# Where the column sums of an arccos attention are taken: ScalarE's accumulator or VectorE

## What is computed

```
cos = jnp.einsum('bhsd,bhtd->bhst', q, k)
g_dist = jnp.arccos(jnp.clip(cos, -1.0 + EPS, 1.0 - EPS)) * SPHERE_RADIUS
attn_score = (1.0 + g_dist / BANDWIDTH ** 0.5) ** (-D_INTRINSIC - ALPHA)
n_r = jnp.sum(attn_score, axis=-1)
n_c = jnp.sum(attn_score, axis=-2)
k_tilde = (n_r ** (-A))[..., :, None] * attn_score * (n_c ** (-A))[..., None, :]
probs = k_tilde / jnp.maximum(jnp.sum(k_tilde, axis=-1, keepdims=True), 1e-12)
out = jnp.einsum('bhst,bhtd->bhsd', probs, v)
```

## Time and profile before

| | us |
|---|---|
| median of 3 runs (5336.09 to 5336.95) | 5336.46 |
| the profiled execution | 5337.28 |
| its span in the trace | 5335.6 |
| ScalarE busy | 4923.4 (92%) |
| VectorE busy | 3274.6 (61%) |
| TensorE matmul busy | 3097.5 (58%) |
| GpSimd busy | 1808.4 (34%) |

### The profile page before, as it was taken

One profiled execution on the slowest core, in us unless ns is written; L12 is line 12 of the kernel. 1 busy time (PEld: TensorE's weight loads), 2 busy tenths in 40 slices (PEclk: granted clock), 3 DMA queues, 4 the chain that ended last, 5 costly groups with the idle time before them and its releaser, 6 DMA issues. The chain is left out here.

```text
span 5335.6 us, 38170 instructions
## 1 busy us (share of the span) xinstructions
PE 3097.5 (58%) x10678; PEld 796.3 (15%) x10678; DVE 3274.6 (61%) x3861; ACT 4923.4 (92%) x2159; POOL 1808.4 (34%) x545
## 2 busy tenths in 40 slices
PE   7635565554444555444546657565655656565699
PEld 4200010000000000000001102111111111111244
DVE  7735665556545565545657676666767576666466
ACT  5799999999999999999989999999999999999521
POOL 0224433444334443334424443344333443334000
PEclk9866655667866656667566857686777668576799
DMA  2100000000000000000000101010010101010200
GB/s 87 63 8 14 18 14 14 14 18 18 14 18 16 12 10 10 6 6 10 12 29 24 36 10 52 2 51 10 30 32 24 36 10 51 7 47 2 82 28 16
DMA packets 71843, 128.14 MB, mean 24 GB/s; under 512 B 9654, under 2 KB 46937, under 8 KB 71706
## 3 DMA queue, kind: packets, MB, share of 16 engines
q1 hardware_dynamic: 70554, 122.50, 7.3%
q0 software_dynamic: 1152, 4.19, 0.3%
HBM read 96.77 MB, written 29.88 MB: 24 GB/s over the span
## 5 line engine op out<-in xcount | busy, mean ns | idle before, releaser
L1114 POOL TENSOR_TENSOR X<-X 128x2048 f32<-128x2048 f32 x504 | 1799.9, 3608 | 3001.3 <-DVE X L928 3001.3
L799 PE MATMUL psum<-stacks 128*128 128x512 bf16 x4096 | 1749.5, 524 | 1397.4 <-DVE X L942 1021.4
L942 DVE TENSOR_TENSOR X<-psum,X 128x1024 f32<-128x1024 f32 x1024 | 1194.3, 1218 | 1057.8 <-ACT X L1146 1046.5
L928 DVE TENSOR_SCALAR X<-psum 128x1024 f32<-128x1024 f32 x1024 | 1186.0, 1215 | 16.6 <-PE psum L799 13.9
L1168 ACT ACTIVATE X<-X 128x2048 f32<-128x2048 f32 x512 | 969.9, 1895 | 6.9
L1146 ACT ACTIVATE X<-X 128x4096 f32<-128x4096 f32 x256 | 904.8, 3604 | 0.7
L1138 ACT ACTIVATE X<-X,consts 128x8192 f32<-128x8192 f32 x128 | 903.7, 7107 | 0.0
L1154 ACT ACTIVATE X<-X 128x4096 f32<-128x4096 f32 (+1 forms) x192 | 897.8, 4739 | 2.7 <-DVE X L942 2.7
L1162 ACT ACTIVATE X<-X,consts 128x16384 f32<-128x16384 f32 x64 | 892.8, 13951 | 0.8
L824 PE MATMUL psum<-X,vp 128*32 128x512 f32 x4096 | 569.2, 715 | 474.1 <-DVE vp L953 473.8
L799 PEld LDWEIGHTS psum<-stacks 128*128 128x128 bf16 x4096 | 260.0, 105 | 2885.0 <-DVE X L942 1847.7
(11 more groups left out here) (165 smaller groups left out, 1347.4 us busy)
## 6 DMA issues: line engine op xcount, KB each, us to landing
V<-expert_w SPq DMA_DIRECT2D x64, 512.0 KB, 3.6
stacks<-qk_parts SPq DMA_DIRECT2D x256, 64.0 KB
qk_parts<-X SPq DMA_DIRECT2D x96, 128.0 KB, 1.9
stacks<-qk_parts SPq DMA_DIRECT2D x64, 192.0 KB
head_out<-evac SPq DMA_DIRECT2D x32, 256.0 KB, 2.1
expert_w<-u_t SPq DMA_DIRECT2D x17, 256.0 KB, 2.6
X<-in_L_attn_x_dram POOLq DMA_DIRECT2D x8, 512.0 KB, 4.3
stacks<-qk_parts SPq DMA_DIRECT2D x32, 128.0 KB
```

What stands on the lines that cost most here:

```text
L799: return nc.tensor.matmul(dst, stacks[:, 1, buf, keys:keys + P], stacks[:, 0, buf, q0:q0 + n], start=True, stop=True)
L928: nc.vector.tensor_scalar(X[:, m % 2, i, j * CW:(j + 1) * CW], ps_cos[j % 2], -CLIP, CLIP, ALU.max, ALU.min).then_inc(cos_ok, 1)
L942: nc.vector.tensor_tensor(part, ps_cos[j % 2], part, ALU.mult).then_inc(cos_ok, 1)
L1114: nc.gpsimd.tensor_tensor(own, own, own, ALU.mult).then_inc(square_ok, 1)
```

## The change

The Exp of the half-heads before the tail (`beside != "tail"`, k = 0 to 7) becomes one instruction for each half of the tiles, 128x8192, without an accumulator. For these half-heads VectorE takes the column sums itself: `values` gets a `reduce_sum` of 4 tiles of 2048 into 4 columns of `ncol`, with a semaphore `sums_ok` behind it for which the reciprocal waits. In the tail the Exp stays as it was; there VectorE raises `sums_ok` by itself, so that the count holds. ScalarE's wait on `vp_ok` stays only in the tail.

```
+        sums_ok = sem("sums_ok")
...
-                def values(k, m, piece):
+                def values(k, m, piece, own):
...
                     dve.wait_ge(score_ok, n * len(EXP_PIECES) + piece + 1)
+                    if own:
+                        nc.vector.reduce_sum(ncol[:, a:b], X[:, m % 2, a:b, :], AX.X).then_inc(sums_ok, 1)
+                    else:
+                        dve.sem_inc(sums_ok, 1)
+                    dve.wait_ge(sums_ok, n * len(EXP_PIECES) + piece + 1)
...
-                        values(k, m, piece)
+                        values(k, m, piece, beside != "tail")
...
-                def scores(k, m):
+                def scores(k, m, beside):
...
                     for piece, (a, b) in enumerate(EXP_PIECES):
-                        wait(act, vp_ok, n * len(EXP_PIECES))
+                        if beside != "tail":
+                            own = tiles(m, a, b)
+                            nc.scalar.activation(own, own, ACT.Exp, scale=POWER).then_inc(score_ok, 1)
+                            continue
+
+                        act.wait_ge(vp_ok, n * len(EXP_PIECES))
                         for i in range(a, b):
...
-                    scores(k, m)
+                    scores(k, m, beside)
```

## The result

The changed kernel takes **5293.62 us** (median of 4 runs, 5292.84 to 5294.67) against 5336.27 for the kernel before (4 runs): a ratio of 0.9919, 95% interval 0.9907 to 0.9932. The forecast was 5295, the range 5289 to 5310. The profiled execution took 5294.67 us, its span 5293.0.

A forecast was written before the change was run, and what follows sets the result against it. ScalarE was taken to bound the kernel before the tail. Saving 1.30 us on each of 32 half-heads, 41.6 us, from 5337.28 gave 5295.7 on the profiled execution, 0.8 above the median, so 5295 us; range 5289 to 5310.

The forecast's parts named there:

- ScalarE bounds the stretch before the tail: Half-heads before the tail: ScalarE busy 2289.69 of 2295.13 us, so a microsecond off its list is one off the time.
- The removed work is 15.15 us a half-head, the added 13.85: ScalarE's Exp before the tail: short Exp and reads occupy 15.15 us, two long Exp 13.85; saving 1.30 us per half-head.
- The third rival: ScalarE's Exp: the accumulator was worth its busy time, 2.62 us saved per half-head, 84 in all, 5253 us; chance 0.02.
- The fourth: Rival on ScalarE's long Exp: a cost stays for each row of 2048, saving 23 us, giving 5313 us; chance 0.02.
- The wait on vp_ok is worth nothing: ScalarE before the tail: no longer waiting on vp_ok gains nothing; all idle time ahead of 512 Exp is 6.9 us.
- A sum takes 8.7 us: VectorE before the tail: each of 64 sums of 8192 elements takes 8.7 us, at 1.04 ns an element.
- the bounds: Limits on one VectorE sum: 8.7 us from the slope between rows, at most 11.0 us if all 0.685 us were per element.
- The sums are hidden, with 3.3 us to spare: VectorE through TensorE to ScalarE's Arctan: products ready for it at E + 40.0 us, its own start at E + 43.3.
- No wait for GpSimd: VectorE's sums beside GpSimd's squares: one-operand sums do not wait; a wait would be 3.5 us, eating 6 us in all.
- The tail stays as it was: Tail: only a semaphore step by VectorE is added; ScalarE's waits there, 17.7 + 6.1 + 2.7 us, stay.
- The rule against tensor_reduce: VectorE's sums: the skill advises against tensor_reduce on a hot path; the prediction held this path is not hot before the tail.

## Why the prediction was right

- **ScalarE bounds the stretch before the tail.** Right: it has 2.8 us of idle time in 2252 there, and a turn lost what ScalarE's list lost.
- **The removed work is 15.15 us a half-head, the added 13.85.** Right to 0.01 us: 13.85 in the timeline. The third rival, which took busy times (2.62 us a half-head), would have given 5253. The fourth, a cost for each row of 2048 in the pattern, falls too: a long Exp takes 7.02 us, like the Arctan of the earlier trace rows.
- **The wait on vp_ok is worth nothing.** Wrong in size. A turn lost 74.04 - 72.66 = 1.38 us, not 1.30, and the 0.08 is the gap between Ln and Exp: 13.98 us now in every turn before the tail, 14.08 in the kernel before in the 28 half-heads inside the loops (13.98 in the four written out). There:

```profile
1527.77 13.95 ACT L1162 ACTIVATE X<-X,consts 128x16384 f32<-128x16384 f32 x1
```

  with the first Exp at 1541.85. The idle time ahead of Exp had stood in the view, 6.9 us for the whole span; I read it as nothing, and some 2.6 us of it went. So the 31 turns lost 2295.13 - 2252.32 = 42.8 us instead of 31 x 1.30 = 40.3. That the whole time fell by 42.7 us, only 1 more than the 41.6 forecast, is in part luck: the rest of the program gave back about 1.5 us, which was not followed up.
- **A sum takes 8.7 us.** Right: 8.678 to 8.687 for all 64. Between the bounds the slope from one row to the next was the good guess, though it joined a sum and a product, two different instructions; the extra sums, 2.28 us for 2048 elements and 4.42 for 4096, now give the same 1.04 ns an element from sums alone.
- **The sums are hidden, with 3.3 us to spare.** Right that they are hidden (the run without them) and right about the place where the room ends, TensorE's additions in front of the third product. The margin was larger than the 3.3 us said: a tile more on each sum, 2.3 us twice, should have made Arctan 1.3 us late and made it 0.24 on average. What was too long in the working is the piece behind the additions and the products after it, priced from rows at the lower clock.
- **No wait for GpSimd.** Right. The one-operand sum does not feel the squares, 8.69 against 8.68 us, while the two-operand product does. That is what the Trainium skill, "SBUF — State Buffer", Who interferes with whom, says of tensor_reduce; the trace now shows it for this shape. By moving the product with V behind the squares the sums even freed it from its waits, which is worth nothing here.
- **The tail stays as it was.** Right within 1 us in its waits: 18.6, 5.8 and 2.5 us against the earlier trace rows.
- **The rule against tensor_reduce.** The Trainium skill, "VectorE: DVE Perf Modes", Rules for kernel authors, has its place where something waits for the sum: the run with all 64 half-heads on VectorE is slower than the kernel before by 113 us, because in the tail VectorE comes to the sums behind its side work. That a sum is VectorE's slowest operation the traces do not show: over 128x512 it takes 0.680 us on average, and a product of two fp32 operands of that shape 0.681 (L407 and L430 of the kernel before). Before the tail the engine had the time free.

## What to carry to other kernels

Take what an engine loses or gains from start to start in the timeline, not from the busy sums: overlapping ends made 16.65 us of busy time only 15.15 us of list. Before work is moved to an idle engine, follow its result through every engine to the next thing that the busy one waits for, and say how late it may be; here that was an addition on TensorE, and the same move that was free in one half of the program cost 155 us in the other. When work is taken off an in-order list, look for the next instruction in it that waits for another engine: the engine only arrives there earlier and waits longer, unless that instruction can be moved down the list.

## What the runs showed of the hardware that I had not expected

- A wait that is always fulfilled is not always free on ScalarE. With a second wait ahead of the first Exp inside a loop, where its value is a register's, Exp starts 0.10 us later (14.08 against 13.98 us from the start of the Ln), shown by putting the wait back alone. In the half-heads written out with constants (n = 1 to 3, 32 to 35 and 60 to 63 of the kernel before) the same wait stands there and the gap is 13.98 to 13.99 us.
- An accumulator read costs ScalarE 0.09 us of its 0.186, and an instruction boundary another 0.09 (14.41 against 15.15 and 13.85 us for a turn's Exp).
- TensorE's additions of one half, the same 32 matmuls, take 3.64 us at a granted clock of 1.00 (the second group of the earlier trace rows), 5.71 at 0.63 after 12.22 us of standing still (the first group), and 6.50 at 0.55 after 7.13 us in the run with two tiles more. With the sums on VectorE they start from rest more often: in the changed kernel TensorE waits ahead of them 182 times, 1369 us in all, in the kernel before 150 times, 827 us.
